# A nine-token first sweep of the recurrence, and operand loads issued ahead of one small store

## The chip, the cores and the metric

One NeuronCore of one Trainium2 chip runs the whole program. The metric is device microseconds of one execution. Engines are named as in the profile: PE (TensorE matmul) and PEld (its weight loads), DVE (VectorE), ACT (ScalarE), POOL (GpSimd), SP (SyncE, which only issues DMAs here).

## What is computed

The input x is 32 images of 32 channels by 16 x 25 = 400 positions. Three blocks follow each other:

1. a graph and temporal convolution block with batch norms, ending in relu(out + x);
2. attention over the 400 tokens of each image with an unusual weighting, softmax(exp(-|q-k|^2)), added to its input;
3. a normalised projection Wx, then a recurrence over the 400 tokens, added to its input:

```
Vt = V.T                                   # V is orthogonal, 32 x 32
def step(yt, wx_t):
    yt = jax.nn.sigmoid(wx_t + yt @ Vt)
    return (yt, yt)
_, ys = jax.lax.scan(step, zeros, swapaxes(Wx, 0, 1))
```

The recurrence is the part that the change touches in its arithmetic.

## The kernel before, in words

Data layout: G = 8 groups of NB = 4 images, so that 4 images x 32 channels fill 128 partitions; a group is a tile of 128 x 400. Groups are handled in PAIRS = 4 pairs (i = 0..3, par = 0, 1; group g = 2i + par).

**Every engine has its own program, written out by hand**, and the programs meet only at semaphores. There is no scheduler: the order of the code of an engine is its order of execution.

**Front stage** (to about 104 us): convolution, then for each pair the keys and queries of attention. ACT (`kq_firsts`, L436) and DVE (`rests`, `parts`, L648 and L659) split keys and queries into bf16 parts in the buffers `kp[par]`, `qp[par]`; POOL (`square_parts`, L345) makes the three "entropy" rows (the squared norms, in parts) in `ep`. One pair of buffers serves all pairs: `kq_firsts` waits at L440 for `kq_stored[par]`, that is for the stores of the pair before to have landed.

**SP's program** moves these parts through DRAM. `store(i)` (L266) waits for `parts_ready` of each group, issues six DMAs of 200 KB for it (`dka` twice, `dqa` twice, `dkb`, `dqb`), twelve for the pair, and then waits for POOL's `e_ready` and issues the 100 KB store of the entropy rows `de` (L280 and L281). `load_operands(i, par)` (L283) loads a group's operands into `ka`, `qa`, `kb`, `qb` [par] with six DMAs (400, 400, 200, 200 KB and two of 9.4 KB). The order is: store(0), both loads of pair 0 (written out), then a hardware loop (`sp.Fori`) of store(1) to store(3), then a second loop of the loads of pairs 1 to 3. In the loops the addresses sit in registers. A load of group g first waits at L314 for the scores of group g - 2, whose buffers it reuses.

**Attention** (about 89 to 190 us): per group, UNITS = 7 units of scores on PE (L980), exp twice on ACT (`inner` L474, `outer` L481), sums of the weights on DVE (L702), the products with V on PE (L1013, L1009). PE's order is fixed by `attend` (L1039): in group g's units it also does group g - 1's products (L1000), which wait at L1005 for `nrm_ready`, DVE's quotient (L718) of group g - 2. Scores of group 0 are woven into the last pair's front stage. At L512 ACT waits, inside group 1 before its third unit, until all stores of `kp`/`qp` parts have landed, because the weights of group 1 (`prob[1]`) overwrite those buffers.

**The recurrence** (206.6 to 228.5 us): the 400 tokens are cut into NC = 40 chunks of L = 10 tokens, all computed at once: 8 groups x 40 chunks = 320 columns, in two halves h of 160 columns. Step s of a half is one matmul by V (L1094) accumulated onto PSUM that already holds the scaled Wx ("seeded" by DVE, `seed`, L786 to L792), and one sigmoid on ACT (L551) from PSUM into `yb[s + 1]`. The first sweep starts every chunk from zero (so its step 0 is only a sigmoid of the seed); then the end of each chunk is shifted by one chunk as the start of the next (`chain`, L794), and the second sweep of ten steps gives the output. DVE compares the ends of the two sweeps (L831 to L837, limit MEET = (2^-18)^2 on the squared difference). If any of the 40,960 values differs by more, a flag is set and NC - 1 = 39 more sweeps run (L572, L842, L1118).

PSUM banks of a half hold the steps in BLOCKS: step 0 in bank 3, steps 1 to 3, 4 to 6, 7 to 9 in banks 0 to 2. DVE seeds the eight blocks of the first sweep in order, and re-seeds a block for the second sweep when `y_ok[h]` says that its steps have been read (L806); the last block is re-seeded after the chain (L812).

Of the kernel before, what the change touches and what calls it, by code (L numbers as in the profile page):

```python
# [40 lines left out]
EPS = 1e-5  # L41
L = 10
NC = N // L
BLOCKS = ((0, 1), (1, 4), (4, 7), (7, 10))
COLS = G * NC
HALF = COLS // 2
FULL = N // P
# [31 lines left out]
def build(nc, x_tok, x, consts, out):  # L79
    with ExitStack() as ctx:  # L80
# [137 lines left out]

        def step_slot(h, s):

            bank, o = (3, 0) if s == 0 else ((s - 1) // 3, SLOT * ((s - 1) % 3))
            return ps[:, 4 * h + bank, o:o + SLOT]

        def block_of(s):

# [34 lines left out]
        def _(sp):  # L260
# [5 lines left out]
            def store(i):  # L266

                for par in range(2):
                    g = 2 * i + par
                    sp.wait_ge(parts_ready, 2 * g + 2)  # L270
                    kpp, qpp = kp[par], qp[par]
                    for scratch, lo, hi, part in (
                            (dka, 0, 2, kpp[:, 0:1].to_broadcast([P, 2, N])),
                            (dka, 2, 4, kpp[:, 1:2].to_broadcast([P, 2, N])),
                            (dqa, 0, 2, qpp[:, 1:3]), (dqa, 2, 4, qpp[:, 1:3]),
                            (dkb, 0, 2, kpp[:, 0:3:2]),
                            (dqb, 0, 2, qpp[:, 0:2])):
                        sp.dma_start(scratch[bass.ds(g, 1), :, N * lo:N * hi].rearrange("o p (s n) -> (o p) s n", n=N),
                                     part).then_inc(kq_stored[par], 16)
                sp.wait_ge(e_ready, i + 1 + CREDIT1)  # L280
                sp.dma_start(de[bass.ds(i, 1)].rearrange("o p n -> p (o n)"), ep[:, 2, :]).then_inc(e_stored, 16)  # L281

            def load_operands(i, par):  # L283

                g = 2 * i + par
                sp.wait_ge(kq_stored[par], 96 * i + 96 + CREDIT_DMA)
                sp.wait_ge(e_stored, 16 * i + 16 + CREDIT_DMA)
                for dst, scratch, n in ((ka, dka, 4), (qa, dqa, 4), (kb, dkb, 2), (qb, dqb, 2)):
                    sp.dma_start(dst[par][0:n * C, :, :], scratch[bass.ds(g, 1)].rearrange(
                        "o (b c) (s n) -> (c s) (o b) n", b=NB, n=N)).then_inc(operands_in[par], 16)  # L290
                rows = de[bass.ds(i, 1)].rearrange("o (g h b r) n -> g h r (o b) n", g=2, h=2, b=NB)
                for h, (dst, row) in enumerate(((kb, 2 * C), (qb, 2 * C + 3))):
                    sp.dma_start(dst[par][row:row + 3, :, :], rows[par, h, 0:3]).then_inc(operands_in[par], 16)
# [10 lines left out]
            for i in range(PAIRS - 1):  # L304
                sp.wait_ge(v_mixed, 2 * i + 2)
                load_tokens(i + 1)
            store(0)
            for par in range(2):
                load_operands(0, par)
            with sp.Fori(1, PAIRS) as i:  # L310
                store(i)
            with sp.Fori(1, PAIRS) as i:
                for par in range(2):
                    sp.wait_ge(s_done, UNITS * (2 * i + par - 1))  # L314
                    load_operands(i, par)

            def store_output(sums):
                for h in range(2):
# [63 lines left out]
        def _(act):  # L382
# [167 lines left out]
            def step(h, s):  # L550
                nc.scalar.activation(y_half(h, s + 1), step_slot(h, s), ACT.Sigmoid).then_inc(y_ok[h], 1)  # L551

            def steps(base):

                for s in range(L):
                    for h in range(2):
                        act.wait_ge(pre[h], base + s)
                        step(h, s)

            for h in range(2):  # L560
                act.wait_ge(seeded[h], 1)
                step(h, 0)
            for s in range(1, L):
                for h in range(2):
                    act.wait_ge(pre[h], s)
                    step(h, s)
            act.wait_ge(cmp_c, 1)
            steps(L)
            act.wait_ge(flag_ok, 1)
            with act.If(act.value_load(flag[0:1, 0:1], min_val=0, max_val=1) != 0):  # L570
                with act.Fori(0, NC - 1) as k:
                    steps(2 * L + L * k)  # L572


        @block.vector
        def _(dve):
# [206 lines left out]
            blink(nc.vector.scalar_tensor_tensor(out=nshf, in0=tot[:, 0:1], scalar=scl, in1=c_("beta"),  # L783
                                                 op0=ALU.mult, op1=ALU.subtract))

            def seed(h, n):  # L786

                lo, hi = BLOCKS[n]
                bank = 4 * h + (3, 0, 1, 2)[n]
                nc.vector.tensor_scalar(ps[:, bank, 0:SLOT * (hi - lo)],  # L790
                                        ul[:, h, lo:hi, :, :].rearrange("p s g c -> p (s g c)"),
                                        scl, nshf, ALU.mult, ALU.subtract).then_inc(seeded[h], 1)  # L792

# [5 lines left out]

            for n in range(len(BLOCKS)):  # L800
                for h in range(2):
                    dve.wait_ge(primed, 1 + PRIME_ORDER.index(4 * h + (3, 0, 1, 2)[n]))
                    seed(h, n)
            for n in range(len(BLOCKS) - 1):
                for h in range(2):
                    dve.wait_ge(y_ok[h], BLOCKS[n][1])  # L806
                    seed(h, n)
            for h in range(2):
                chain(h, L)
            nc.vector.tensor_copy(ys, yb[:, L, :, :]).then_inc(cmp_c, 1)  # L810
            for h in range(2):
                seed(h, len(BLOCKS) - 1)  # L812
# [12 lines left out]
                                            by_step(t0[:, 4 * h:4 * h + 4, :], L - 1),  # L825
                                            y_half(h, L), ALU.add).then_inc(added, 1)

            add_residual(L)

            dve.wait_ge(cmp_c, 1)  # L830
            nc.vector.tensor_tensor(yd, yb[:, L, :, :], ys, ALU.subtract).then_inc(cmp_c, 1)  # L831
# [8 lines left out]
            with dve.If(dve.value_load(flag[0:1, 0:1], min_val=0, max_val=1) != 0):  # L840
                dve.wait_ge(primed, len(PRIME_ORDER) + 1)
                with dve.Fori(0, NC - 1) as k:  # L842
                    for h in range(2):
                        chain(h, 2 * L + L * k)
                        for n in range(len(BLOCKS)):
                            seed(h, n)
                for h in range(2):
                    dve.wait_ge(y_ok[h], 2 * L + L * (NC - 1))
                dve.wait_ge(out_done, 16 * (G // OUT_G))
                add_residual(2 * L + L * (NC - 2))  # L850


        @block.tensor
        def _(pe):
# [238 lines left out]
            def step(h, s):  # L1093
                mm_(step_slot(h, s), c_("vT"), y_half(h, s), start=False, stop=True,  # L1094
                    skip_group_check=True).then_inc(pre[h], 1)

            def steps(sweep):
                for s in range(L):
                    for h in range(2):
                        pe.wait_ge(seeded[h], len(BLOCKS) * sweep + block_of(s) + 1)  # L1100
                        if s == 0:
                            pe.wait_ge(start_ok[h], sweep)
                        else:
                            pe.wait_ge(y_ok[h], L * sweep + s)
                        step(h, s)

            for s in range(1, L):
                for h in range(2):
                    pe.wait_ge(seeded[h], block_of(s) + 1)
                    pe.wait_ge(y_ok[h], s)  # L1110
                    step(h, s)
            steps(1)
            pe.wait_ge(cmp_c, 4)
# [108 lines left out]
```

## Time and profile before

| | |
|---|---|
| median of 3 runs | 237.83 us (237.70 to 238.28) |
| profiled execution, own time | 237.66 us |
| its span, first to last instruction | 235.8 us |
| granted TensorE clock, mean | 0.956 of 2.4 GHz |
| PE busy | 199.2 us (85%) |
| ACT busy | 169.9 us (72%) |
| DVE busy | 157.7 us (67%) |
| POOL busy | 27.5 us (12%) |
| data moved by DMA | 26.83 MB, 14.74 read from and 11.88 written to HBM |

The span leaves out 237.66 - 235.8 = 1.9 us around it. A busy share is an average over three stages with different limits, so the table alone does not say what a change in one stage is worth. For that one reads the chain of waits (which operation released the next), the timeline of each engine with the idle time in front of an instruction and its releaser, and the windows view, which gives each engine's busy time in a stretch.

### The profile page before, as it was taken

The page shows a single profiled execution, that of the slowest core. Times are in us where ns is not written, and L with a number is a line of the kernel's source. Part 1 is how long each engine was busy: PE and PEld are TensorE (multiplying, and loading weights), DVE is VectorE, ACT ScalarE, POOL GpSimd, SP SyncE. Part 2 cuts the span into 40 slices and gives each one's busy share as a digit, 9 for nine tenths or more (in the row PEclk, how much of TensorE's full clock was granted, in tenths as well). Part 3 has the DMA queues.
Part 4 walks back from the last instruction along what each step waited for, and adds up shares of the span by engine and source line. Part 5 has one row for each costly group of instructions (what it writes and reads, how often), then busy time and mean ns, then how long its engine had stood idle before and what let it go on. Part 6 is the DMA issues. An engine that isn't in the chain of part 4 may idle for free. (4 is left out here: it accounts for less than half of the span.)

```text
span 235.8 us, 3561 instructions
## 1 busy us (share of the span) xinstructions
PE 199.2 (85%) x1110; PEld 94.1 (40%) x1110; DVE 157.7 (67%) x296; ACT 169.9 (72%) x309; POOL 27.5 (12%) x44
## 2 busy tenths in 40 slices
PE   0775998898899797959989999999999998588950
PEld 0552554464465353523333343434343333245630
DVE  0417618965992992399578577777869695595880
ACT  4028179579759959797998999999899984365640
POOL 6000000054024006016100101010101000000000
PEclk9997699999999999997999999999999999889985
DMA  6940020039599709348880716162520000000016
GB/s 173 372 126 0 0 72 1 0 77 348 160 273 285 221 0 308 129 138 296 212 215 0 192 23 190 22 169 47 176 37 0 3 0 0 0 3 0 0 51 233
DMA packets 26883, 26.83 MB, mean 114 GB/s; under 512 B 1550, under 2 KB 25806, under 8 KB 26740
## 3 DMA queue, kind: packets, MB, share of 16 engines
q1 hardware_dynamic: 26868, 26.64, 38.6%
q8 instruction: 8, 0.13, 0.2%
q14 instruction: 7, 0.06, 0.1%
HBM read 14.74 MB, written 11.88 MB: 113 GB/s over the span
## 5 line engine op out<-in xcount | busy, mean ns | idle before, releaser
L474 ACT ACTIVATE arena<-ps 128x800 f32<-128x800 f32 (+1 forms) x56 | 44.5, 796 | 6.5 <-PE ps L980 4.9
L481 ACT ACTIVATE arena<-arena 128x800 f32<-128x800 f32 (+1 forms) x56 | 46.3, 829 | 0.0
L980 PE MATMUL ps<-qa,ka 128*128 128x400 bf16 (+1 forms) x128 | 35.8, 343 | 3.6 <-ACT arena L474 3.6
L980 PE MATMUL ps<-qb,kb 96*128 96x400 bf16 (+1 forms) x128 | 35.7, 341 | 0.0
L702 DVE TENSOR_TENSOR psum<-arena 128x400 f32<-128x400 f32 x32 | 19.6, 612 | 13.5 <-ACT arena L481 13.4
L702 DVE TENSOR_TENSOR psum<-psum,arena 128x400 f32<-128x400 f32 x32 | 19.5, 609 | 7.2 <-ACT arena L481 5.8
L1013 PE MATMUL ps<-arena,vb 128*32 128x400 f32 x192 | 21.0, 513 | 0.8 <-issue 0.8
L905 PE MATMUL ps<-arena,cst 128*128 128x400 f32 x32 | 15.7, 620 | 6.5 <-DVE arena L627 6.5
L980 PEld LDWEIGHTS ps<-qa,ka 128*128 128x128 bf16 (+1 forms) x128 | 10.4, 98 | 26.9 <-ACT arena L474 10.0
L1094 PE MATMUL ps<-yb,cst 128*128 128x160 f32 x76 | 17.2, 335 | 2.2 <-ACT yb L551 1.3
L711 DVE RECIPROCAL arena<-ps 128x400 f32<-128x400 f32 x7 | 18.6, 2651 | 0.0
L551 ACT ACTIVATE yb<-ps 128x160 f32<-128x160 f32 x40 | 12.0, 303 | 8.5 <-PE ps L1094 6.6
L627 DVE COPY arena<-arena 32x400 f32<-32x400 f32 x48 | 17.2, 358 | 0.9
L645 DVE TENSOR_TENSOR arena<-ps,arena 128x400 f32<-128x400 f32 x8 | 4.2, 569 | 17.2 <-ACT arena L434 17.2
L419 ACT ACTIVATE t<-arena,small 128x400 f32 (+1 forms) x8 | 4.8, 629 | 14.0 <-DVE arena L637 14.0
L1094 PEld LDWEIGHTS ps<-yb,cst 128*128 128x128 f32 x76 | 11.3, 188 | 8.6 <-issue 5.0
L350 POOL TENSOR_TENSOR arena<-arena,cst 128x400 bf16<-128x400 f32 x4 | 4.6, 1147 | 86.4 <-ACT arena L453 86.4
L980 PEld LDWEIGHTS ps<-qb,kb 96*128 96x128 bf16 (+1 forms) x128 | 10.5, 99 | 9.5 <-issue 5.4
L399 ACT ACTIVATE arena<-ps,small 128x400 f32<-128x400 f32 x8 | 5.4, 683 | 10.6 <-PE ps L891 10.6
L905 PEld LDWEIGHTS ps<-arena,cst 128*128 128x128 f32 x32 | 6.1, 224 | 15.8 <-DVE arena L627 14.5
L360 POOL COPY vb<-vst 128x384 f32 (+1 forms) x8 | 4.1, 516 | 62.5 <-PE ps L1009 62.5
L406 ACT ACTIVATE arena<-ps,small 96x400 f32<-96x400 f32 (+1 forms) x16 | 10.8, 676 | 0.6 <-PE ps L896 0.4
(137 smaller groups left out, 357.4 us busy)
## 6 DMA issues: line engine op xcount, KB each, us to landing
dka<-arena SPq DMA_DIRECT2D x16, 200.0 KB, 3.1
dqa<-arena SPq DMA_DIRECT2D x16, 200.0 KB, 3.2
ka<-dka SPq DMA_DIRECT2D x8, 400.0 KB
qa<-dqa SPq DMA_DIRECT2D x8, 400.0 KB
arena<-x_tok SPq DMA_DIRECT2D x4, 400.0 KB
t<-x SPq DMA_DIRECT2D x1, 1600.0 KB, 12.1
dkb<-arena SPq DMA_DIRECT2D x8, 200.0 KB, 3.5
dqb<-arena SPq DMA_DIRECT2D x8, 200.0 KB, 4.6
```

What stands on the lines that cost most here:

```text
L399: nc.scalar.activation(y4[par], ps[:, 2 * par + 1, 0:N], ACT.Relu, bias=bn_h2[:, S_GC:S_GC + 1], scale=bn_s2[:, S_GC:S_GC + 1]).then_inc(y ...
L406: last = nc.scalar.activation(zp[par][lo:hi, PAD:PAD + N], ps[lo:hi, 2 * par, 0:N], f, bias=bn_h2[lo:hi, S_Z:S_Z + 1], scale=bn_s2[lo:hi, ...
L474: nc.scalar.activation(prob[par][:, lo:hi, :], ps[:, o:o + hi - lo, 0:N], ACT.Exp, scale=2.0).then_inc(e1_done, 1)
L481: nc.scalar.activation(p, p, ACT.Exp).then_inc(p_ready, 1)
L551: nc.scalar.activation(y_half(h, s + 1), step_slot(h, s), ACT.Sigmoid).then_inc(y_ok[h], 1)
L627: last = nc.vector.tensor_copy(*tap_input(par, j, k))
L702: nc.vector.tensor_tensor(dst, a, prob[par][:, t, :], ALU.add).then_inc(part_sum, 1)
L711: nc.vector.reciprocal(rden, ps[:, 5, 0:N]).then_inc(rden_ready, 1)
L905: mm_(ps[:, 2 * par + 1, 0:N], cst[:, o + P * j:o + P * j + P], tap_in[par][j], start=(j == 0), stop=False)
L980: last = mm_(ps[row:row + keys, bank, 0:N], kk[par][0:rows, b, o:o + keys], qq[par][0:rows, b, :], start=first, stop=not first, skip_group ...
L1013: mm_(ps[C * b:C * b + C, 4, 0:N], vb[:, par, P * k + C * b:P * k + C * b + C], prob[par][:, FULL * b + k, :], start=(k == 0), stop=False, ...
L1094: mm_(step_slot(h, s), c_("vT"), y_half(h, s), start=False, stop=True, skip_group_check=True).then_inc(pre[h], 1)
```

## The change

Two edits, independent of each other.

**1. The recurrence.** SKIP = 1: the first sweep starts each chunk at its second token, so it has nine tokens: a sigmoid of the seed of step 1, then steps 2 to 9. The second sweep keeps all ten steps. The blocks become (0, 2), (2, 5), (5, 8), (8, 10), so that bank 3 holds steps 0 and 1; in the first sweep its seed covers step 1 alone (`first`). All waits that count steps go down by SKIP.

**2. SP's order.** The store of the entropy rows is a function of its own (`store_e`), the loops over pairs are written out, and the loads of group 2 (pair 1, par 0) come between the twelve part stores of the last pair and its `store_e`. Everything else of SP keeps its order.

```
-BLOCKS = ((0, 1), (1, 4), (4, 7), (7, 10))
+BLOCKS = ((0, 2), (2, 5), (5, 8), (8, 10))
+SKIP = 1
...
+            bank, o = (3, SLOT * s) if s < 2 else ((s - 2) // 3, SLOT * ((s - 2) % 3))
             return ps[:, 4 * h + bank, o:o + SLOT]
+        def step_slots(h, lo, hi):
+            bank, o = (3, SLOT * lo) if lo < 2 else ((lo - 2) // 3, 0)
+            return ps[:, 4 * h + bank, o:o + SLOT * (hi - lo)]
...
+            def store_e(i):
                 sp.wait_ge(e_ready, i + 1 + CREDIT1)
                 sp.dma_start(de[bass.ds(i, 1)].rearrange("o p n -> p (o n)"), ep[:, 2, :]).then_inc(e_stored, 16)
...
-            store(0)
-            for par in range(2):
-                load_operands(0, par)
-            with sp.Fori(1, PAIRS) as i:
+            def load_next(i, par):
+                sp.wait_ge(s_done, UNITS * (2 * i + par - 1))
+                load_operands(i, par)
+            for i in range(PAIRS - 1):
                 store(i)
-            with sp.Fori(1, PAIRS) as i:
-                for par in range(2):
-                    sp.wait_ge(s_done, UNITS * (2 * i + par - 1))
-                    load_operands(i, par)
+                store_e(i)
+                if i == 0:
+                    for par in range(2):
+                        load_operands(0, par)
+            store(PAIRS - 1)
+            load_next(1, 0)
+            store_e(PAIRS - 1)
+            load_next(1, 1)
+            for i in range(2, PAIRS):
+                for par in range(2):
+                    load_next(i, par)
...
             for h in range(2):
                 act.wait_ge(seeded[h], 1)
-                step(h, 0)
-            for s in range(1, L):
+                step(h, SKIP)
+            for s in range(SKIP + 1, L):
                 for h in range(2):
-                    act.wait_ge(pre[h], s)
+                    act.wait_ge(pre[h], s - SKIP)
                     step(h, s)
             act.wait_ge(cmp_c, 1)
-            steps(L)
+            steps(L - SKIP)
...
-            def seed(h, n):
-                lo, hi = BLOCKS[n]
-                bank = 4 * h + (3, 0, 1, 2)[n]
-                nc.vector.tensor_scalar(ps[:, bank, 0:SLOT * (hi - lo)],
+            def seed(h, n, first=0):
+                lo, hi = max(BLOCKS[n][0], first), BLOCKS[n][1]
+                nc.vector.tensor_scalar(step_slots(h, lo, hi),
...
-                    dve.wait_ge(y_ok[h], BLOCKS[n][1])
+                    dve.wait_ge(y_ok[h], BLOCKS[n][1] - SKIP)
                     seed(h, n)
             for h in range(2):
-                chain(h, L)
+                chain(h, L - SKIP)
...
-            for s in range(1, L):
+            for s in range(SKIP + 1, L):
                 for h in range(2):
                     pe.wait_ge(seeded[h], block_of(s) + 1)
-                    pe.wait_ge(y_ok[h], s)
+                    pe.wait_ge(y_ok[h], s - SKIP)
                     step(h, s)
```

## Rows read from the trace of the kernel before

**Rows 1.** Windows view, one stretch of attention: us, then busy us (instructions) per engine.

```profile
130.00:142.00 12.00, 12.00 (x82) 4.58 (x74) 8.12 (x11) 11.38 (x18) 1.06 (x3) 1.00 0.41 105
```

**Rows 2.** Chain of waits, tail: start us, us, what.

```profile
206.66 2.17 DVE ps L790 x4
...
208.87 0.55 PE ps L1094 x2
...
209.45 0.31 ACT yb L551
...
209.90 0.52 PE ps L1094 x2
...
216.86 0.52 PE ps L1094 x2
...
217.41 0.31 ACT yb L551
```

**Rows 3.** Timeline of DVE, tail: start, us, line, operation, [idle before it <- releaser].

```profile
214.09 1.46 DVE L790 TENSOR_SCALAR ps<-ul,small 128x480 f32<-128x480 f32 x2 [0.49 <-ACT yb L551]
...
217.07 0.24 DVE L797 COPY yb<-yb 128x156 f32<-128x156 f32 x1 [1.52 <-ACT yb L551]
```

**Rows 4.** Timeline of ACT, 86 to 130 us.

```profile
98.86 0.49 ACT L442 CAST arena<-ps 128x400 bf16<-128x400 f32 x1 [1.17 <-DMA dqb<-arena]
...
111.90 0.84 ACT L474 ACTIVATE arena<-ps 128x800 f32<-128x800 f32 x1 [1.27 <-DMA dqb<-arena]
...
119.31 0.84 ACT L474 ACTIVATE arena<-ps 128x800 f32<-128x800 f32 x1 [0.21 <-PE ps L980]
```

**Rows 5.** Timelines of PEld, DVE and PE, 118 to 121 us.

```profile
118.35 0.10 PEld L980 LDWEIGHTS ps<-qa,ka 128*128 128x128 bf16 x1 [1.33 <-DMA qb<-de]
...
119.79 0.57 DVE L718 TENSOR_TENSOR sq<-ps,arena 128x400 f32<-128x400 f32 x1
...
120.46 0.88 PE L1013 MATMUL ps<-arena,vb 128*32 128x400 f32 x8 [0.56 <-issue]
```

**Rows 6.** Timeline of SP's queue: DMA issues, 50 to 115 us.

```profile
50.08 0.93 SPq L278 DMA_DIRECT2D dka<-arena  x2
...
56.79 0.62 SPq L278 DMA_DIRECT2D dqb<-arena  x1
...
87.96 0.95 SPq L278 DMA_DIRECT2D dka<-arena  x2
...
94.57 0.54 SPq L278 DMA_DIRECT2D dqb<-arena  x1
...
102.85 0.95 SPq L278 DMA_DIRECT2D dka<-arena  x2
...
109.43 0.53 SPq L278 DMA_DIRECT2D dqb<-arena  x1
...
110.34 0.34 SPq L281 DMA_DIRECT2D de<-arena  x1
...
111.36 0.42 SPq L289 DMA_DIRECT2D ka<-dka  x1
```

**Rows 7.** DMA view: last store of groups 1, 5, 7 (size, us to landing).

```profile
dqb<-arena SPq DMA_DIRECT2D x1, 200.0 KB, 5.0
...
dqb<-arena SPq DMA_DIRECT2D x1, 200.0 KB, 4.2
...
dqb<-arena SPq DMA_DIRECT2D x1, 200.0 KB, 2.4
```

**Rows 8.** DMA view of 95 to 99 us, queue of instruction fetches (count, MB, share).

```profile
q8 instruction: 1, 0.02, 2.3%
```

**Rows 9.** Windows view, middle (last two columns: DMA share, GB/s).

```profile
97.00:98.00 1.00, 1.00 (x7) 0.49 (x6) 0.78 (x2) 0.69 (x2) 0.00 (x0) 1.00 0.05 8
...
103.75:111.50 7.75, 5.33 (x29) 1.68 (x30) 7.47 (x10) 6.83 (x12) 4.61 (x4) 0.78 0.97 329
...
110.00:111.00 1.00, 1.00 (x8) 0.35 (x10) 0.97 (x2) 0.63 (x1) 0.18 (x1) 1.00 1.04 351
```

More of the change, by code:

```diff
@@ L219, in step_slot @@
         def step_slot(h, s):
-            bank, o = (3, 0) if s == 0 else ((s - 1) // 3, SLOT * ((s - 1) % 3))
+            bank, o = (3, SLOT * s) if s < 2 else ((s - 2) // 3, SLOT * ((s - 2) % 3))
             return ps[:, 4 * h + bank, o:o + SLOT]
+        def step_slots(h, lo, hi):
+            bank, o = (3, SLOT * lo) if lo < 2 else ((lo - 2) // 3, 0)
+            return ps[:, 4 * h + bank, o:o + SLOT * (hi - lo)]
         def block_of(s):
@@ L571, in _ @@
                 with act.Fori(0, NC - 1) as k:
-                    steps(2 * L + L * k)
+                    steps(2 * L - SKIP + L * k)
         @block.vector
@@ L802, in _ @@
                     dve.wait_ge(primed, 1 + PRIME_ORDER.index(4 * h + (3, 0, 1, 2)[n]))
-                    seed(h, n)
+                    seed(h, n, SKIP)
             for n in range(len(BLOCKS) - 1):
                 for h in range(2):
-                    dve.wait_ge(y_ok[h], BLOCKS[n][1])
+                    dve.wait_ge(y_ok[h], BLOCKS[n][1] - SKIP)
                     seed(h, n)
             for h in range(2):
-                chain(h, L)
+                chain(h, L - SKIP)
             nc.vector.tensor_copy(ys, yb[:, L, :, :]).then_inc(cmp_c, 1)
@@ L826, in add_residual @@
                                             y_half(h, L), ALU.add).then_inc(added, 1)
-            add_residual(L)
+            add_residual(L - SKIP)
             dve.wait_ge(cmp_c, 1)
@@ L843, in _ @@
                     for h in range(2):
-                        chain(h, 2 * L + L * k)
+                        chain(h, 2 * L - SKIP + L * k)
                         for n in range(len(BLOCKS)):
@@ L847, in _ @@
                 for h in range(2):
-                    dve.wait_ge(y_ok[h], 2 * L + L * (NC - 1))
+                    dve.wait_ge(y_ok[h], 2 * L - SKIP + L * (NC - 1))
                 dve.wait_ge(out_done, 16 * (G // OUT_G))
-                add_residual(2 * L + L * (NC - 2))
+                add_residual(2 * L - SKIP + L * (NC - 2))
         @block.tensor
@@ L1103, in steps @@
                         else:
-                            pe.wait_ge(y_ok[h], L * sweep + s)
+                            pe.wait_ge(y_ok[h], L * sweep - SKIP + s)
                         step(h, s)
-            for s in range(1, L):
+            for s in range(SKIP + 1, L):
                 for h in range(2):
                     pe.wait_ge(seeded[h], block_of(s) + 1)
-                    pe.wait_ge(y_ok[h], s)
+                    pe.wait_ge(y_ok[h], s - SKIP)
                     step(h, s)
```

## Prediction

> **What bounds the kernel now.** I read the windows view first, then the chain of waits, then the timelines of ACT, PE, DVE and SP's queue around each wait on a DMA. From about 120 us to 190 us TensorE has no gap: in a typical stretch of 12 us it is busy for all 12.00, in the order written in `attend` [rows 1]. So that stretch can't be shortened by this change, only started earlier. What the change can touch lies in two places: the tail, where the recurrence runs as a strict alternation of matmul, sigmoid, matmul [rows 2], and the middle, where ACT twice stands waiting for a store of SP, 1.17 us in front of 98.86 (call it stall A) and 1.27 us in front of 111.90 (stall B) [rows 4].
>
> **The recurrence, what goes.** A step of a half is a matmul of 0.52, the start of the sigmoid, 0.31, and 0.14 until the next matmul. The matmul of the second half starts at 209.90 for step 2 and at 216.86 for step 9 [rows 2]: (216.86 - 209.90) / 7 = 0.994 us a step. The first sweep has one step fewer, and the halves overlap, so one step leaves the chain once: **-0.99 us**. The step that goes is a plain one: before, the sigmoid of the seed is step 0 and nine matmul steps follow; after, it is step 1 and eight follow.
>
> **The recurrence, what could be late next.** The start doesn't move: the first sweep's first seed covers 160 columns as before, the second block three steps as before, so the first matmul still waits for the fourth seed (2.17 us for four seeds, matmul at 208.87) [rows 2]. Blocks 2 and 3 then have one step more of time before PE wants them than they had. The seeds and re-seeds of blocks 0 and 3 change width (320 columns in place of 480 or 160) and cancel but for tenths; that is hidden behind the steps, as DVE is idle in between. The re-seed of block 2 is the tight one: it waits for seven sigmoids, before and after, and starts at 214.09 in both; it takes 1.46 us for two, so DVE is free at 215.55. The chain copy at 217.07, in front of which DVE was idle for 1.52 us, comes at 216.08 after, with 0.53 us of idle time left [rows 3]. So the step is not given back. The second sweep, the comparison and the output stores keep their form and shift by 0.99.
>
> **The comparison.** Nine tokens in place of ten leave a larger gap between the two sweeps' chunk ends. I worked it out from the reference's formulas and inputs, with the recurrence started from zero n tokens ahead of each chunk end: the largest of all values is 3.1e-7 for ten tokens, 1.25e-6 for nine, 6.1e-6 for eight. The limit is 2^-18 = 3.8e-6. Nine stays under it by a factor of 3, which leaves little to the rounding of the chip.
>
> **SP's order: the loads of group 2.** They move from behind the entropy store to in front of it. What moves: six issues (first at 111.36) go ahead of one 100 KB issue at 110.34 and of POOL's `e_ready`; the last part store is issued at 109.43 and takes 0.53, so the loads can start at about 110.0, 1.3 us earlier [rows 6]. Their own wait (scores of group 0) has long been met. Behind them on SP stands only the entropy store of the last pair, then at about 113.7; its readers are the loads of the last pair, some 40 us later, and POOL doesn't write that buffer again. What the earlier landing is worth is read from PE: it waits for these operands until 118.35, but its next group of products starts at 120.46, and that one is set by the quotient on DVE, 119.79 + 0.57 = 120.36 [rows 5], which hangs on ACT's exps since 111.90 by way of the reciprocal. From 120.46 on PE is full. ACT itself waited for group 2's scores for only 0.21 us [rows 4], and its next exp but two needs scores that stand behind those products. So I take **0 us** for the moved loads, with 0.2 as the bound of a gain. The cover is the quotient: had it come 1 us earlier, the loads would be worth 1 us, and this edit takes that wait away in advance. As a loss: the loads' reads now run behind the last part store, where the entropy store ran; if they slowed its landing the price would be at stall B, a tenth or two.
>
> **SP's order: the loops written out.** This is the part whose price the trace doesn't show, and both stalls hang on it. Stall A ends with the landing of the last part store of pair 2 (issued 94.57, landing 4.2 later), stall B with that of pair 3 (109.43 + 2.4 = 111.83) [rows 6, 7]. Both stand on one chain: A delays DVE's parts of the last pair, these start SP's stores at 102.85, their landing is B, B sets 120.36, and from there PE is full. Each tenth that SP gains or loses in either counts to the end. In the loop, SP's issues have register work between them; stores of the last pair take 102.85 to 109.43 to reach the last one, 6.58 us. Written out, the stores of pair 0 took 50.08 to 56.79, 6.71 us [rows 6]. That row says: nothing gained (a loss of 0.1). But their last store needed 5.0 us to land, against 2.4 in the last pair [rows 7], so they went into a fuller queue; in the last pair the DMA engines moved 329 GB/s on average and 351 in a full stretch [rows 9], so a quicker issue can win 7.75 x (1 - 329/351) = 0.49 us at most for a pair of groups. I take 0.3 for each of the two, between 0 and 0.49 and nearer to the bandwidth's bound since the last pair is the stretch concerned: **-0.6 us**, ends +0.1 and -1.0.
>
> Stall A has a cliff beside it. The same store lands after 2.4 us in pair 3 and after 4.2 in pair 2 [rows 7]. In pair 2 nearly all data were through by 97 us (97 to 98 us: 8 GB/s, share 0.05) [rows 9], and the one other thing there is a fetch of 16 KB of instructions [rows 8]: one of the DMA engines seems to have been held by it, with its part of the store behind. With 2.4 us the landing would be at 96.97, before ACT is ready at 98.86 - 1.17 = 97.69. So if the stores get ahead of the fetch, all of A goes: -1.17 in place of -0.3. [...] If the fetch were free here, A would be a matter of issue alone and there would be no cliff. [...]
>
> **Sum.** The profiled execution took 237.66 us, 1.86 of it around the span of 235.8; it lies 0.17 below the median 237.83, and I make the sum against it and add it to the median: -0.99 - 0.6 = -1.59, so 236.2.
>
> **Rivals.**
> 1. *Only the recurrence pays.* The DMA engines, not SP's issue, set both landings; for it speaks that written-out issue at 50 us was no faster [rows 6] and a share of 0.97 [rows 9]. 237.83 - 0.99 = 236.85.
> 2. *Stall A goes as a whole.* The stores pass the fetch. -0.99 - 1.17 - 0.3 to -0.5: 235.3. It needs 0.6 us or so in pair 2, more than the 0.49 of the bandwidth, so it is less likely.
> 3. *Slower: stores written out land late.* Pair 0, the only written-out one, took from first issue to last landing 56.79 + 5.0 - 50.08 = 11.7 us, pair 3 in the loop 109.43 + 2.4 - 102.85 = 9.0, pair 2 10.8 [rows 6, 7]. If this is due to the form and not to the time of the kernel, B grows by 2.7 and A by 0.9: +3.6 - 0.99, 240.4. It outweighs the recurrence from 1.0 us on. Against it: the slow landings of pair 0 begin with its first store, when other traffic had just been there.
> 4. *The step is hidden.* DVE's re-seeding runs 0.53 us later than I count and the chain copy waits for it: the gain shrinks by what exceeds that; 236.8 to 237.3.
> 5. *The edit doesn't do what it says: the flag is set.* 39 sweeps of ten steps of 0.994: +388 us, about 625 us. The factor of 3 speaks against it.
>
> **How the numbers follow.** Forecast (recurrence and some of SP's issue) 0.50, its own range 235.7 to 236.7; rival 1 0.22; rival 2 0.13; rival 3 0.09; rival 4 0.04; rival 5 0.02. The range 235.0 to 237.3 takes in all of the forecast, rival 1 and rival 4 and most of rival 2, and leaves out rivals 3 and 5. A measurement of this kernel can tell about 0.3%, 0.71 us, from no change: faster is below 237.12. Forecast, rival 2 and nearly all of rival 1 are faster, 0.84; rival 4, the edge of rival 1 and the mild end of rival 3 are no change, 0.07; the rest of rival 3 and rival 5 slower, 0.09.
>
> **What would show it.** Recurrence: chain copy at its new place with about 0.5 us idle in front of it on DVE, eight steps of 0.99 between first and last matmul of the first sweep where there were nine. Loads: first load of group 2 within 0.1 us of the last part store's issue, no wait of PE for operands at group 2, and the wait for the quotient longer instead. Loops: issues of pair 3 in less than 6.58 us from first to last, stall A and B below 1.17 and 1.27; for rival 1 both unchanged, for rival 2 no wait for a DMA near 98, for rival 3 landings of 4 to 5 us. The prediction is wrong if the fetch or SP's own fetches fall elsewhere, or if TensorE's full stretch doesn't start earlier although B ends earlier.

## The result and the profile after

The changed kernel took **236.24 us**, median of 20 runs (233.72 to 240.01), the kernel before 238.36 us beside it, median of 20 (235.88 to 241.10). The ratio of the two is **0.9913, interval 0.9887 to 0.9940**: faster by 0.87%, 2.07 us of 238.36. Both kernels spread over some 6 us from run to run, a good deal more than the three runs shown before the change let one expect; the runs left out as disturbed are not in the ratio. The profiled execution took 233.72 us with a span of 231.9 us and a mean granted clock of 0.983.

The span is 3.9 us shorter than in the profile before, twice what the ratio says. So the first thing to do is to cut both profiles at the same events. The cuts: SP's first store of pair 2, PE's first products among the units of group 2 (the ones that wait for the quotient of group 0), DVE's first seed, the chain copy of the first half, the end.

| stage, us | before | after | difference |
|---|---|---|---|
| 1: start to first store of pair 2 | 87.96 | 85.16 | -2.80 |
| 2: to the products in group 2's units | 32.50 | 31.81 | -0.69 |
| 3: to the first seed | 86.20 | 86.16 | -0.04 |
| 4: first seed to chain copy | 10.41 | 10.39 | -0.02 |
| 5: chain copy to the end | 18.73 | 18.38 | -0.35 |

Stage 1 is not the change's, but for 0.14 us. The same four matmuls of the front stage, first in the profile before, then in that after (timeline of PE, then the windows view of 20 to 30 us, whose column of 0.66 or 1.00 is the granted clock):

```profile
21.24 3.04 PE L905 MATMUL ps<-arena,cst 128*128 128x400 f32 x4 [2.90 <-DVE arena L627]
...
20.00:30.00 10.00, 8.76 (x45) 4.99 (x45) 7.76 (x19) 3.82 (x7) 0.00 (x0) 0.66 0.01 2
```

```profile
20.16 1.70 PE L922 MATMUL ps<-arena,cst 128*128 128x400 f32 x4 [2.90 <-DVE arena L645]
...
20.00:30.00 10.00, 8.86 (x52) 4.96 (x53) 7.30 (x17) 4.13 (x8) 0.00 (x0) 1.00 0.11 23
```

Before, TensorE was granted 0.50 of its full clock for 6.8 of these 10 us (20.5 to 27.3); the four matmuls took 3.04 us in place of 1.70. The profile gives the clock only as a share of the full one: where two expectations below write 1.2 GHz it shows 0.50. Matmuls of 480 columns follow each other at 0.20 us where the share is 1.00 (ten in 2.19 us, the last of them 0.37 long) and at 0.40 where it is 0.50 (six in 2.61, the last 0.61 long; both further down), which is 2.4 and 1.2 columns a ns. The 2.4 and 1.2 GHz of the texts on record are these rates read as frequencies, an estimate. Most of the 2.80 us is there already at SP's first store of pair 0, 50.08 before ([rows 6]) and 47.42 after, and the stores of pair 0 were written out in both kernels:

```profile
47.42 0.91 SPq L284 DMA_DIRECT2D dka<-arena  x2
```

SP's edit acts from the stores of pair 1 on, so a little of stage 1 is its own. From the first store of pair 0 to the first of pair 2 the profiles of all kernels of this study with loops took 37.87 to 37.89 us (five profiles), those with the loops written out 37.73 to 37.74 (eight): a gain of 0.14 us that the prediction did not count and whose path was not traced. The rest of stage 1 varies by itself: without the kernel with a long padding it took 86.5 to 89.0 us in the other kernels. One profile against one profile can't tell 2 us here; stages can.

Stage 2, the middle. Timelines of SP's queue and of ACT, PEld, DVE and PE, after, and the landing of the last store of pairs 2 and 3:

```profile
85.16 0.88 SPq L284 DMA_DIRECT2D dka<-arena  x2
...
90.99 0.63 SPq L284 DMA_DIRECT2D dqb<-arena  x1
...
98.78 0.89 SPq L284 DMA_DIRECT2D dka<-arena  x2
...
104.04 0.53 SPq L284 DMA_DIRECT2D dkb<-arena  x1
...
105.00 0.33 SPq L284 DMA_DIRECT2D dqb<-arena  x1
...
105.46 0.38 SPq L298 DMA_DIRECT2D ka<-dka  x1
...
108.41 0.84 ACT L492 ACTIVATE arena<-ps 128x800 f32<-128x800 f32 x1 [1.79 <-DMA dqb<-arena]
...
113.82 0.10 PEld L997 LDWEIGHTS ps<-qa,ka 128*128 128x128 bf16 x1 [1.33 <-DMA qb<-de]
...
113.86 0.33 PE L997 MATMUL ps<-qa,ka 128*128 128x400 bf16 x1 [0.95 <-ACT arena L492]
...
116.30 0.57 DVE L736 TENSOR_TENSOR sq<-ps,arena 128x400 f32<-128x400 f32 x1
...
116.97 0.88 PE L1030 MATMUL ps<-arena,vb 128*32 128x400 f32 x8 [1.20 <-issue]
...
dqb<-arena SPq DMA_DIRECT2D x1, 200.0 KB, 3.0
...
dqb<-arena SPq DMA_DIRECT2D x1, 200.0 KB, 3.3
```

There is no ACT wait for a DMA in pair 2 any more (1.17 us in [rows 4]). In pair 3 the same wait grew from 1.27 to 1.79 us. The loads of group 2 start at 105.46, right behind the last part store; PE starts on group 2's scores 3.15 us ahead of the products (113.82 and 116.97), before 2.11 ([rows 5]), and the wait ahead of the products grew from 0.56 to 1.20 us. Whether the moved loads did that is a question for the experiments.

Stage 4, the first sweep. Chain of waits and timeline of DVE, after, then the windows view of the stage:

```profile
205.34 0.55 PE ps L1111 x2
...
206.36 4.28 PE ps L1111 x14
...
210.65 0.98 PE ps L1111 x4
...
211.64 0.98 PE ps L1111 x4
...
212.64 0.53 PE ps L1111 x2
...
213.52 0.24 DVE L814 COPY yb<-yb 128x156 f32<-128x156 f32 x1 [0.53 <-ACT yb L569]
...
203.13:213.52 10.39, 8.59 (x33) 5.74 (x32) 8.39 (x14) 5.80 (x18) 0.00 (x0) 0.84 0.01 2
```

It has one step fewer and lasts as long as before. From 206.36 on 14 matmuls take 4.28 us; from 210.65 on the steps run at 0.99 again as in [rows 2]. The granted clock of the stage is 0.84: (1 - 0.84) x 2 x 10.39 = 3.3 us at half the full clock (the windows view has 0.50 for 206.8 to 210.2), and the slow matmuls say that they lay inside the steps. In the profile before there was such a fall too; the windows view of its stage 4 has 0.92, 1.7 us, and the chain shows steps of 0.99 from the start ([rows 2]), so it was over when the steps began.

```profile
206.66:217.07 10.41, 8.95 (x40) 5.60 (x38) 8.39 (x15) 6.40 (x20) 0.00 (x0) 0.92 0.01 2
```

So this profile hides the gain of the recurrence, and an experiment has to show it. The chain copy came behind 0.53 us of idle time of DVE.

### The profile page after: what moved, and what is told of

Read it like the earlier page. It is cut to its first block and busy times, and to the rows that moved or that the text cites. A ratio compares the mean times of both kernels' runs of the same rounds, so it can differ in the third digit from the quotient of the medians.

```text
span 231.9 us, 3393 instructions
## 1 busy us (share of the span) xinstructions
PE 194.5 (84%) x1106; PEld 91.6 (40%) x1106; DVE 157.4 (68%) x296; ACT 169.2 (73%) x307; POOL 27.6 (12%) x44
## 5 line engine op out<-in xcount | busy, mean ns | idle before, releaser
L997 PE MATMUL ps<-qa,ka 128*128 128x400 bf16 (+1 forms) x128 | 35.0, 337 | 3.3 <-ACT arena L492 3.3
L997 PE MATMUL ps<-qb,kb 96*128 96x400 bf16 (+1 forms) x128 | 34.9, 334 | 0.0
L1111 PE MATMUL ps<-yb,cst 128*128 128x160 f32 x72 | 17.9, 362 | 2.7 <-DVE ps L807 1.5
L922 PE MATMUL ps<-arena,cst 128*128 128x400 f32 x32 | 13.6, 547 | 7.5 <-DVE arena L645 7.5
L569 ACT ACTIVATE yb<-ps 128x160 f32<-128x160 f32 x38 | 11.4, 304 | 8.9 <-PE ps L1111 7.2
L424 ACT ACTIVATE arena<-ps,small 96x400 f32<-96x400 f32 (+1 forms) x16 | 10.8, 677 | 0.6 <-PE ps L913 0.4
L922 PEld LDWEIGHTS ps<-arena,cst 128*128 128x128 f32 x32 | 4.8, 188 | 16.4 <-DVE arena L645 16.4
```

Of the source, the lines that this page charges most:

```text
L424: last = nc.scalar.activation(zp[par][lo:hi, PAD:PAD + N], ps[lo:hi, 2 * par, 0:N], f, bias=bn_h2[lo:hi, S_Z:S_Z + 1], scale=bn_s2[lo:hi, ...
L922: mm_(ps[:, 2 * par + 1, 0:N], cst[:, o + P * j:o + P * j + P], tap_in[par][j], start=(j == 0), stop=False)
L997: last = mm_(ps[row:row + keys, bank, 0:N], kk[par][0:rows, b, o:o + keys], qq[par][0:rows, b, :], start=first, stop=not first, skip_group ...
```

## Experiments

Each stage below is cut as in the table above. Stage 2 is where the forecast gain of SP's edit lies, stage 4 where the recurrence's does.

**The two edits apart.** Four kernels, timed beside the kernel before.

The recurrence alone: all of the diff but SP's program.

> The recurrence's edit alone, SP's program as before. My theory: -0.99 us, one step of 0.994, so a ratio of 0.996; middle unchanged, with ACT's two waits for the last part stores at 1.2 and 1.3 us. Rival theory (TensorE's clock eats the step): in the profile after, the first sweep took 8.18 us from its first matmul of the second half to the chain copy against 8.20 before, because steps ran at half clock; then the gain is anywhere between 0 and 0.99 from execution to execution, and the median shows about half of it or less.

SP's edit alone:

> SP's edit alone (loops written out and the loads of group 2 moved), recurrence as before. My theory: the gain of the middle, -0.6 to -0.9 us (1.17 of the wait in pair 2 goes, some 0.6 comes back in the last pair), ratio 0.997. Rival (middle is neutral, the recurrence is the whole gain): ratio 1.000.

SP's loops written out, the loads where they were; against the kernel above this is

```
             store(PAIRS - 1)
-            load_next(1, 0)
             store_e(PAIRS - 1)
+            load_next(1, 0)
             load_next(1, 1)
```

> SP's loops written out, but the loads of group 2 stay behind the entropy store; recurrence as before. My theory: all of SP's gain is here, the same time as with the moved loads within 0.2 us; ACT doesn't wait for a DMA in pair 2. Whether the last part store still lands 3.3 us after its issue tells what made the wait in the last pair longer: 3.3 if it is the written-out issue, 2.4 if it is the loads directly behind it.

And the order alone, addresses in registers:

```
+            with sp.Fori(PAIRS - 1, PAIRS) as i:
+                store(i)
+            with sp.Fori(1, 2) as i:
+                load_next(i, 0)
+            with sp.Fori(PAIRS - 1, PAIRS) as i:
+                store_e(i)
```

> The loads of group 2 in front of the last entropy store, but SP's addresses stay in registers (loops of one pass where needed); recurrence as before. My theory: no change, within 0.2 us of before: ACT's wait in pair 2 stays at 1.2 us, PE gets group 2's operands some 1 us earlier and waits for the quotient instead. Rival (the move itself is what pays or costs): a gain of up to 1 us, or a longer wait of ACT in the last pair.

| kernel | ratio to before | interval | stage 2 | stage 4 |
|---|---|---|---|---|
| recurrence alone | 0.9976 | 0.9925 to 1.0027 | 32.79 | 10.43 |
| SP's edit alone | 0.9976 | 0.9936 to 1.0016 | 31.82 | 11.13 |
| loops written out alone | 0.9947 | 0.9902 to 0.9991 | 31.79 | 11.40 |
| order alone, in loops | 1.0028 | 0.9990 to 1.0066 | 33.35 | 11.13 |

The ratios are too wide to part effects of 0.2 to 0.4%; three of the four cannot be told from no change. The stages part them. *Stage 2*: with the loops written out it lasts 31.8 us whether the loads are moved (31.82) or not (31.79), and 32.5 to 32.8 with loops. So the gain is the writing out, and the moved loads are worth nothing, as forecast. The last part store of pair 3 lands late without the moved loads too. From the kernel with written-out loops alone, the landing in the DMA view and the timelines of ACT and PE:

```profile
dqb<-arena SPq DMA_DIRECT2D x1, 200.0 KB, 3.3
...
110.49 0.84 ACT L486 ACTIVATE arena<-ps 128x800 f32<-128x800 f32 x1 [1.77 <-DMA dqb<-arena]
...
115.95 0.34 PE L992 MATMUL ps<-qa,ka 128*128 128x400 bf16 x1 [0.97 <-DMA qb<-de]
```

So it is not the loads behind it. Here PE waits for the operands until 115.95, where with the moved loads the profile names ACT (113.86 above); but counted from the first store of pair 2 both are at 28.7 us (115.95 - 87.26 and 113.86 - 85.16), and the wait ahead of the products is 1.20 us in both. The longer wait for the quotient is not the moved loads' either: it is 1.20 us in the six profiles in which TensorE's clock did not fall in stage 2, and 0.21 to 0.61 in the seven in which it did.

The order alone had a stage 2 of 33.35. Its profiled execution was a long one (240.30 us, where the median of that kernel is 238.18), with TensorE at 0.50 of its clock for 6.8 us from 106.9 on and busy for all of the 12 us from 108.99. Up to the first store of pair 3 it took 15.18 us, as the recurrence alone did with its loops (15.22). It also turned out no clean test of the last pair: in its loops of a single pass, SP issued the last store of pair 3 5.95 us behind the first, nearly as in written-out code.

*Stage 4*: the kernel with ten tokens and 3.4 us of fallen clock inside the steps (loops written out) took 11.40 us, the ones with nine tokens and as much of it 10.43 (recurrence alone) and 10.39 (changed kernel): -1.0. The row of the recurrence alone, and the windows view that shows the fall:

```profile
215.93 0.24 DVE L802 COPY yb<-yb 128x156 f32<-128x156 f32 x1 [0.49 <-ACT yb L557]
...
205.50:215.93 10.43, 7.82 (x32) 5.73 (x32) 8.43 (x15) 5.69 (x18) 0.00 (x0) 0.84 0.01 2
```

```profile
216.60 0.24 DVE L809 COPY yb<-yb 128x156 f32<-128x156 f32 x1 [1.52 <-ACT yb L563]
...
205.20:216.60 11.40, 9.54 (x37) 6.35 (x36) 8.40 (x14) 6.42 (x20) 0.00 (x0) 0.85 0.01 1
```

**What made ACT wait in pair 2.** Two theories: the fetch of 16 KB of instructions that ran at 95.9 us, 7.9 us behind SP's first store of pair 2, or the backlog of the stores themselves. The kernel before, with 24 semaphore increments that nobody waits for at the head of PE's program, to bring the fetch into the middle of those stores:

```
             pe.sem_inc(e_ready, CREDIT1)
+            for _ in range(24):
+                pe.sem_inc(pad, 1)
```

> [...] My theory (the fetch holds one DMA engine and the stores behind it land late): stores issued before the fetch land after 2.1 to 2.4 us, all issued after it after 4 us or more, and ACT's wait in pair 2 stays near 1.2 us. Rival theory (the queue's own backlog makes the last one late): only the last store, at 4.2, is late, as before.

And the same with 240 in place of 24, to have the fetch behind the last of those stores:

> [...] My theory: the last part store lands after 2.4 to 3 us, ACT's wait in pair 2 goes although SP's loops are as before, and the stretch from the first store of pair 2 to the products of group 2 (32.5 us before) shrinks by about 1.2. Rival (written-out issue is what removes the wait): the landing stays at 4.2 and the wait at 1.2.

With 24, the DMA view around the fetch, SP's queue, and the landings of the stores issued at 89.75 and 94.71:

```profile
q8 instruction: 1, 0.02, 5.5%
...
89.75 0.54 SPq L279 DMA_DIRECT2D dqb<-arena  x1
...
90.59 2.21 SPq L279 DMA_DIRECT2D dka<-arena  x2
...
dqb<-arena SPq DMA_DIRECT2D x1, 200.0 KB, 4.1
...
dqb<-arena SPq DMA_DIRECT2D x1, 200.0 KB, 2.7
...
97.45 0.49 ACT L443 CAST arena<-ps 128x400 bf16<-128x400 f32 x1 [0.85 <-DMA dqb<-arena]
```

The fetch is now at 91.2 us, 4.3 behind the first store of pair 2, and the store that is late is now the one issued at 89.75: 4.1 us. SP itself was held: two issues took 2.21 us, where the same two took 0.96 in the profile before. The last one landed after 2.7, but as SP issued it later, ACT still waited for 0.85 us. I had expected all stores behind the fetch to land late; instead SP's issues were held for part of the delay. The rival, that only the last store is late, failed too.

With 240, where the fetch comes at 128.1, 10.6 us behind the first store of pair 2, and the last part store of pair 2 was issued at 124.09:

```profile
q8 instruction: 1, 0.02, 5.7%
...
124.09 0.54 SPq L279 DMA_DIRECT2D dqb<-arena  x1
...
dqb<-arena SPq DMA_DIRECT2D x1, 200.0 KB, 2.3
...
140.22 0.84 ACT L475 ACTIVATE arena<-ps 128x800 f32<-128x800 f32 x1 [1.40 <-DMA dqb<-arena]
```

It lands after 2.3 us, ACT has no wait for a DMA in pair 2, the one of pair 3 is still there (1.40, before 1.27), and stage 2 lasts 31.29 us, 1.21 less than before, with SP's loops in place. (The padding itself cost some 30 us at the start, a span of 264.9 us for 235.8; only the stages count.) So the wait in pair 2 is the fetch's. Counted from the first store of pair 2, the fetch starts 7.9 us later in all three kernels with loops and PE's program in its place (95.89 - 87.96 before, 94.44 - 86.54 with the recurrence alone, 96.89 - 88.99 with the order alone), and a last part store issued at 6.61 that took 2.4 would land at 9.0: it is caught. Written out, the store is issued at 5.83 (85.16 to 90.99), lands some 8.8 us behind the first issue, and the fetch starts at 8.3 to 8.6. That most of its data are ahead of the fetch by then is my reading, from the landing after 3.0 us, as with no fetch near it in pair 3 below. Why the fetch itself comes 0.4 later there I don't know. The faster issue by itself brought the landing no nearer: with 240 and loops it is 6.60 + 2.3 = 8.9 us behind the first issue.

**What made it wait longer in pair 3.** In the changed kernel an 8 KB fetch runs at 106.5 that was at 80.2 before. The changed kernel with 40 idle instructions early in SP's program:

```
             sp.wait_ge(zeroed, 8)
+            for _ in range(40):
+                sp.sem_inc(pad, 1)
```

> The changed kernel, with 40 increments of an unused semaphore on SP early on, where SP waits anyway. In the changed kernel a fetch of 8 KB runs at 106.5 us, 1.5 us behind SP's issue of the last part store of pair 3, which lands after 3.3 us and came 0.4 us late; in the kernel before that fetch ran at 80 us. The padding moves it into an idle stretch of SP. Theory 1 (SP's fetch makes the last store of pair 3 late): no gap ahead of its issue, landing 2.4 to 2.9, ACT's wait 1.79 down to 1.2 or so, stretch from the first store of pair 2 to the products of group 2 down from 31.8 to about 31.2. Theory 2 (SP issues faster than the 16 DMA engines move, the queue only fills): landing stays above 3, last landing 9.5 us after the first issue of pair 3, stretch unchanged.

```profile
q14 instruction: 1, 0.01, 4.7%
...
102.49 0.89 SPq L285 DMA_DIRECT2D dka<-arena  x2
...
108.34 0.61 SPq L285 DMA_DIRECT2D dqb<-arena  x1
...
dqb<-arena SPq DMA_DIRECT2D x1, 200.0 KB, 3.1
...
111.49 0.84 ACT L495 ACTIVATE arena<-ps 128x800 f32<-128x800 f32 x1 [1.16 <-DMA dqb<-arena]
```

The fetch has gone to 72 us, so it is SP's own. The last store is issued 5.85 us behind the first (6.22 in the changed kernel, with a gap of 0.43 us ahead of it), lands 8.95 us behind the first issue (9.5), ACT waits 1.16 us, and stage 2 lasts 31.16 us. The landing of the last store is still 3.1 us behind its issue, not 2.4: both theories hold a share. SP issues faster, and the last landing is no earlier for it: from first issue to last landing 8.98 before, 8.95 here.

**Both stalls in all profiles.** Stage 2, cut once more at SP's first store of pair 3, in us (the kernel with six matmuls and three of the four in the last row are described below):

| kernels | pair 2 to pair 3 | pair 3 to the products |
|---|---|---|
| loops, PE's fetch at 7.9 (before, recurrence alone) | 14.89, 15.22 | 17.61, 17.58 |
| loops, PE's fetch earlier (24) | 14.57 | 17.60 |
| loops, PE's fetch moved behind (240) | 13.62 | 17.67 |
| written out, SP's fetch behind the last stores (changed kernel, SP's edit, written out alone, six matmuls) | 13.62 in all four | 18.19, 18.20, 18.17, 18.10 |
| written out, SP's fetch moved away (four profiles) | 13.61 to 13.62 | 17.55 to 17.64 |

The first column is 13.6 us wherever PE's fetch does not meet the stores, in loops too; the second is 17.6 wherever SP's fetch does not, written out or not. The one exception is the order alone (15.18 and 18.17), whose second figure has no fetch of SP in it but 6.8 us of fallen clock. A fall of 3.4 us explains neither column: TensorE's clock fell for that long in stage 2 with six matmuls (18.10) and not in the changed kernel (18.19), and in one of the two profiles of SP's padding (17.55) and not in the other (17.64).

**Timed, and TensorE's clock.** The same kernel in more rounds:

> The changed kernel with the same 40 padding increments on SP as in e7, now timed. In e7's profile the stretch from the first store of pair 2 to the products of group 2 was 31.2 us, against 31.8 in the changed kernel and 32.5 before. My theory: a gain of 0.6 us on the changed kernel, so a ratio to before of about 0.989 where the changed kernel had 0.9913. Rival: the padding only moves the fetch to another place that costs as much, ratio 0.991 to 0.993.

**235.22 us, ratio 0.9851, 0.9809 to 0.9894.** Stage 2 31.26 us in its profile. Lower than the changed kernel's 0.9913 by 0.6%, though the intervals overlap; what shows the gain is the stage, 31.16 to 31.26 us in four profiles with SP's padding and 31.72 to 31.82 in four without.

For the clock, six matmuls without use between the ones that prime the banks:

```
-            for bank in PRIME_ORDER[:-1]:
+            for bank in PRIME_ORDER[:-2]:
                 prime(bank)
+            for _ in range(6):
+                mm_(ps[:, 6, 0:PRIMED], ka[0][:, 0, 0:P], ...)
+            prime(PRIME_ORDER[-2])
```

> The changed kernel, with six more matmuls of 480 columns without use between the ones that prime the banks, so that PE isn't idle for 1.5 us ahead of the recurrence. Theory: in the profile after, TensorE fell to 1.2 GHz for 3.4 us inside the first sweep, behind that idle stretch, and the sweep took 8.18 us from its first matmul of the second half to the chain copy where 7.2 were expected. If keeping PE busy avoids the fall: a first sweep of 7.2 us and a gain of up to 1 us against the changed kernel, ratio to before 0.988. Rival: the fall is decided by the longer idle time before the priming, it stays, and the six matmuls cost up to 1 us where they run at half clock.

Ratio 0.9886, 0.9818 to 0.9955, not to be told from the changed kernel's. The six matmuls and the windows view of their stretch:

```profile
205.13 2.61 PE L1108 MATMUL ps<-ka 128*128 128x480 bf16 x6
...
204.00:208.00 4.00, 4.00 (x13) 1.64 (x12) 3.26 (x9) 2.28 (x5) 0.00 (x0) 0.57 0.00 0
```

The clock had fallen before they began (204.3 us), they took 2.61 us, and the first step came 2.80 us behind the first seed in place of 1.53; stage 4 lasted 10.58 us. The fall stayed and the six cost time, as the rival said.

Then ten such matmuls in bank 7 further up, in the idle time ahead of the batch norm's small matmul, with SP's padding:

```
+            pe.wait_ge(u2_ready, G - 2)
+            for _ in range(10):
+                mm_(ps[:, 7, 0:PRIMED], ka[0][:, 0, 0:P], ...)
             pe.wait_ge(bn_c, 2)
```

> e10 with ten matmuls of 480 columns without use in PE's idle 2.8 us ahead of the batch norm's small matmul. Theory: TensorE's granted clock then doesn't fall to 1.2 GHz around the first sweep, whose nine tokens take 9.4 us from the first seed to the chain copy, in place of 10.4 (3.4 us of fallen clock inside) or 11.4 (6.8 us): 1 to 2 us faster than e10, ratio 0.982. Rival: the fall comes all the same and the ten matmuls at 0.4 us each delay the small matmul by up to 1 us.

And both together:

> e11 with the six matmuls of e8 as well, so that PE is busy from the last projection to the recurrence's first step. Theory: as e11, and if idle time ahead of the first step is what counts, this one keeps the clock and e11 doesn't. Rival: as in e8, the six delay the first step by 1.3 us where they run at half clock, and what the clock gives back is spent.

```profile
199.16 2.19 PE L1107 MATMUL ps<-ka 128*128 128x480 bf16 x10
...
203.00:216.00 13.00, 9.89 (x46) 6.32 (x44) 10.83 (x22) 8.06 (x24) 0.00 (x0) 1.00 0.00 0
...
213.50 0.24 DVE L817 COPY yb<-yb 128x156 f32<-128x156 f32 x1 [0.53 <-ACT yb L572]
```

With the ten: **233.62 us, ratio 0.981, 0.976 to 0.986**, the fastest kernel of this study. The clock is 1.00 throughout the sweep and stage 4 lasts 9.41 us, which is the 10.41 of before (whose fall was over when the steps began) less one step. With both: 235.03 us, 0.9869, 0.9831 to 0.9906, stage 4 9.41 as well, so the six add nothing there. Stage 4 of the kernel with SP's padding alone was 9.41 too, as its fall (3.4 us from 203.6) ended ahead of the steps; in the other profile of that same kernel (the one above, with the fetch at 72 us) 6.8 us of fallen clock lay in the steps, and stage 4 took 11.41. The intervals of 0.9851 and 0.981 overlap: that the ten matmuls gain anything in the median isn't shown, only that in their two profiles the clock did not fall there.

**How far the first sweep can be cut.** Two tokens skipped:

```
-BLOCKS = ((0, 2), (2, 5), (5, 8), (8, 10))
-SKIP = 1
+BLOCKS = ((0, 3), (3, 6), (6, 9), (9, 10))
+SKIP = 2
```

(The two functions that place the steps in the banks follow.)

> The changed kernel with two tokens skipped (first sweep of eight, blocks of 3, 3, 3, 1). By the working from the reference the largest difference is then 6.1e-6 against the limit of 3.8e-6: the flag is set and 39 more sweeps of ten steps run, at 0.994 us a step +388 us, so about 620 us, a little more for the second output. If the working is wrong and eight tokens are enough on the chip: 235.2 us, one more step of 0.99 off.

816.48 us. The flag is set, as worked out. The price was mis-sized: (816.5 - 236.2) / 39 = 14.9 us a sweep in place of 9.94. The chain of waits in 300 to 316 us shows why, as does the clock in the windows view:

```profile
304.88 0.24 DVE yb L814
...
305.12 0.51 DVE ps L807
...
306.40 1.12 DVE ps L807 x2
...
307.66 0.70 DVE ps L807
...
300.00:450.00 150.00, 118.19 (x413) 85.18 (x412) 51.79 (x100) 61.89 (x206) 0.00 (x0) 0.74 0.00 0
```

In the flag's loop the next sweep's first matmul (308.40) comes 3.5 us behind the last sigmoid (304.85), and DVE shifts and seeds in between: that is where the seeds are not hidden. The rest of the 4.9 us was not taken apart; the steps also run slower than 0.994 us each, with TensorE granted 0.74 of its clock over these 150 us.

## Why the prediction was right, and where it wasn't

Forecast 236.2 us, measured 236.24; forecast -1.6 us, measured -2.07 with an interval of -2.7 to -1.4. That the time itself was met to 0.04 us is luck: the kernel before measured 238.36 beside it, not 237.83, and that made up for the larger gain. The profiles show -0.69 for the middle, at the same clock -1.0 for the sweep, and -0.14 ahead of the middle, so -1.8.

- **One step of 0.99, not given back.** Right, in size and mechanism. 11.40 against 10.43 and 10.39 with 3.4 us of fallen clock in the steps, 10.41 against 9.41 with none in them. DVE's idle time ahead of the chain copy is 0.53 us, the number worked out. What the prediction left out is that the sweep's length hangs on when TensorE's clock falls, by as much as the step or twice it.
- **The moved loads: 0.** Right in number: with or without the move stage 2 is 31.8 us, and the loads start 0.46 us behind the last part store's issue. Of the reason, that the quotient sets the products, the trace bears out the rule (DVE's quotient ends at 116.87, the products start at 116.97), but the longer wait for it was no effect of the move: it is 1.20 us with and without. Nor did PE start on group 2's scores earlier: with the loads moved it was released by ACT at the same 28.7 us.
- **Writing out the loops: -0.3 at each stall.** The sum came out by luck (-0.69 for -0.6): both terms were wrong, by about as much up as down. Stall A went as a whole: -1.17 in place of -0.3; that was rival 2's half, with 0.13. The step of it that failed was that a quicker issue wins by an earlier landing, up to the bandwidth's bound of 0.49 us: SP got 0.8 us ahead in pair 2 (5.83 for 6.61), but where no fetch meets the last store it lands no earlier for that (8.9 us behind the first issue in loops, 8.8 written out). What it won is the fetch: 8.8 in place of 10.8. I had made the bound from the mean rate of pair 3 and had not asked how far ahead of the fetch the last store's data needed to be. Stall B grew by 0.52 in place of shrinking by 0.3. Here the failed step is that SP's program has fetches of its own, which the text had only as a last clause on what would prove it wrong, and by that clause it was: written out, SP's 8 KB fetch fell behind the last stores. With it moved away, stall B is 1.16 to 1.24, which is before's 1.27: the faster issue bought nothing in pair 3, as rival 1 said of both.
- **The fetch as the cause of stall A.** Argued then from one row of instruction DMA, now shown: moved with 24 instructions another store was late, moved behind the stores none was. None of the profiles names a fetch as what PE itself waited for; the store issued 1.3 us ahead of it (94.57 and 95.9) landed after 4.2 us in place of 2.4, 1.8 us later.
- **Rival 3, stores written out land late.** In pairs 2 and 3 they landed after 3.0 and 3.3 us, not after 5. A small part of it was real: in pair 3, without SP's fetch, -0.7 in issue against +0.7 in landing.
- **The comparison.** Nine tokens are enough and eight aren't, as worked out. The price of the flag was low by a third (9.94 us a sweep for 14.9): it was taken from a sweep whose seeds are hidden and whose steps ran at the full clock.

What stays open: by what path the written-out loops gain 0.14 us ahead of pair 2; whether the clock's falls differ in number between the kernels; why PE's fetch comes 0.4 us later with SP written out; and what of the last 0.2 us between ratio (-2.07) and stages (-1.8) is noise. The interval holds both.

## What to carry to other kernels

When two profiles differ by more than the times do, cut them at events that the change can't move against each other, and compare stage by stage; a single span carries the luck of the clock (here 3.9 us between the spans, 2.07 by the ratio). A wait for a DMA that lands later than its neighbours of the same size is worth a look at what else used the DMA engines, and that includes instruction fetches, here PE's and SP's: 24 or 240 idle instructions on PE and 40 on SP moved them, and stage 2 became shorter by 0.3, 1.2 and 0.6 us. A forecast that comes out in the sum can still be wrong in each term, and only the stages tell. The step taken off the strict chain paid in full (1.0 us for a step of 0.99) while its helper engine kept idle time (DVE, 0.53 us), and that idle time could be read beforehand.

## What the runs showed of the hardware

- A fetch of 16 KB of PE's instructions in pair 2 took 1.0 to 1.9 us, and a store of 200 KB issued around it landed after 4.1 to 4.6 us, where the same store took 2.3 with the fetch moved behind it. SP's issue was held around it too: two issues took 2.21 us in place of 0.96.
- Padding PE's program moved a fetch of 16 KB (q8 of the page of before: eight, 0.13 MB): from 7.9 us behind the first store of pair 2 to 4.3 with 24 instructions, to 10.6 with 240. Padding SP's moved one of 8 KB (q14: seven, 0.06 MB), from 106.5 to 72.2 us with 40.
- TensorE's granted clock fell to 0.50 of the full one for 3.4 or 6.8 us in or ahead of the first sweep in every profile but the two with ten added matmuls in the 2.8 us of idle time before; the nine-token sweep lasts 9.41, 10.4 or 11.41 us by it. Six matmuls behind that idle time, with the fall begun, took 0.43 us each, where the ten took 0.22, and the clock fell all the same.
- SP's written-out issues are faster (twelve stores: last issue 5.8 us behind the first, for 6.6), but the last one then takes 0.7 to 0.8 us longer to land (3.0 and 3.1 to 3.2, for 2.3 and 2.4), so the last landing stays some 8.9 us behind the first issue.
